# One core, a chain of graph layers: the fetch of sums by source moves from the 23rd to the 37th of 52 groups of row puts, and the K network's way back asks for its tiles from the 40th group on

## What is computed

```python
def get_H(xx):
    z = xx @ W_fc.T
    e = sigmoid(concatenate([z[src], z[dst]], -1) @ W_attn.T)
    w = exp(e - segment_max(e, dst)[dst])
    h = segment_sum(w / segment_sum(w, dst)[dst] * z[src], dst)
    h1 = segment_sum((h @ W_encK.T + b_encK)[src], dst)
    K = _mlp3(h1, ...)                                   # a row for each node
    ue = (h @ W_p1.T + b_p1)[src] + (h @ W_p2.T + b_p2)[dst]
    U = _mlp3(ue, ...)                                   # a row for each edge
    return sum(segment_sum(K[src] * U, dst))
dHdx = jax.grad(get_H)(x)
return dHdx @ J.T - dHdx @ D.T
```

## Time and profile before

| what | us |
|---|---|
| median of 3 runs | 10295.42 |
| lowest and highest | 10291.75, 10301.3 |
| profiled execution, its span | 10295.6 |
| POOL waiting for DVE's join within the puts | 100.26 |
| stretch of the dh1 tiles, first issue to last matmul | 8341.82 to 8866.6 |
| stretch of dsum, first load to the join on PE | 8878.37 to 9073.24 |

### The profile page before, as it was taken

How to read it: one execution, slowest core, us unless ns; L and a number is a source line. 1 busy time by engine, 2 the same in 40 slices (tenths; PEclk the granted TensorE clock), 3 DMA queues, 4 the chain that set the end, 5 groups by cost and what they waited for, 6 DMA issues and landing times. The chain is left out here.

```text
span 10295.6 us, 89257 instructions
## 1 busy us (share of the span) xinstructions
PE 4966.0 (48%) x33607; PEld 2470.1 (24%) x33607; DVE 4608.8 (45%) x6086; ACT 2834.9 (28%) x2203; POOL 6485.8 (63%) x6251
## 2 busy tenths in 40 slices
PE   1000039992467777752666553343330044239955
PEld 0000028882122222210222211233320021023322
DVE  5678777772000010001999400677764410448920
ACT  0111100000000000000999400555556400449910
POOL 4777767776777737777888777787777477310000
PEclk5555555555679999875999866666665566569977
DMA  5666559999999999993655694455559879849978
GB/s 181 226 221 221 183 89 352 350 348 351 405 381 416 386 402 386 385 416 133 201 183 192 232 383 168 161 186 178 178 209 381 310 269 364 316 162 368 359 315 362
DMA packets 987471, 2910.75 MB, mean 283 GB/s; under 512 B 198168, under 2 KB 547467, under 8 KB 936824
## 3 DMA queue, kind: packets, MB, share of 16 engines
q1 hardware_dynamic: 753570, 2579.72, 65.6%
q0 software_dynamic: 213744, 171.38, 6.7%
q10 hardware_dynamic: 19814, 155.07, 3.9%
HBM read 2027.96 MB, written 877.74 MB: 282 GB/s over the span
## 5 line engine op out<-in xcount | busy, mean ns | idle before, releaser
L650 PE MATMUL ps<-arena 128*32 128x400 f32 (+2 forms) x12200 | 2075.4, 694 | 1512.6 <-DMA arena<-cells_w 808.6
L827 PE MATMUL ps<-arena 128*33 128x400 f32 x6400 | 1146.9, 510 | 486.8 <-DVE arena L820 479.3
L650 PEld LDWEIGHTS ps<-arena 128*32 128x32 f32 (+1 forms) x12200 | 629.6, 150 | 2951.7 <-issue 1423.6
L459 POOL DMA_INDIRECT cells_t<-arena x832 | 1081.7, 1300 | 299.6 <-issue 299.6
L456 POOL DMA_INDIRECT arena<-t_a,arena x832 | 953.7, 1146 | 253.5 <-issue 253.5
L459 POOL DMA_INDIRECT cells_c<-arena x832 | 819.8, 985 | 421.4 <-issue 291.4
L459 POOL DMA_INDIRECT cells_w<-arena x832 | 812.1, 976 | 302.9 <-issue 302.9
L459 POOL DMA_INDIRECT sorted<-arena x832 | 808.1, 971 | 301.0 <-issue 301.0
L459 POOL DMA_INDIRECT xd<-arena x832 | 824.5, 991 | 258.2 <-issue 253.3
L456 POOL DMA_INDIRECT arena<-t_kv,idx x832 | 816.8, 982 | 257.9 <-issue 253.3
L668 DVE COPY carry<-ps 64x128 f32<-64x128 f32 (+1 forms) x5 | 1.5, 296 | 1851.0 <-PE ps L650 1851.0
(11 more groups left out here) (526 smaller groups left out, 8221.1 us busy)
## 6 DMA issues: line engine op xcount, KB each, us to landing
arena<-cells_w SPq DMA_DIRECT2D x250, 3200.0 KB
arena<-cells_c SPq DMA_DIRECT2D x100, 3200.0 KB
cells_w<-arena SPq DMA_DIRECT2D x50, 3200.0 KB
cells_c<-arena SPq DMA_DIRECT2D x50, 3200.0 KB
cells_t<-arena SPq DMA_DIRECT2D x50, 3200.0 KB
arena<-cells_c SPq DMA_DIRECT2D x100, 1600.0 KB
arena<-cells_t SPq DMA_DIRECT2D x100, 1600.0 KB
arena<-cells_t SPq DMA_DIRECT2D x50, 3200.0 KB
```

The costliest lines, as they stand in the source:

```text
L459: return pool.indirect_dma_start(table, bass.IndirectOffsetOnAxis(ap=index, axis=0), source, None)
L650: mm = pe.matmul(bank[base + k][g * f:(g + 1) * f, 0:m], rows_of, tile[:, g * width + at:g * width + at + m], start=first, stop=last, skip ...
L827: last = pe.matmul(bank[4 * kind + 2 * h + c][64 * g:64 * g + 33, 0:400], own[:, t, :], moving[:, at:at + 400], start=t == 0, stop=t == NT ...
```

## The change

Two lines change. On POOL the block of step 4 (one joining fetch, one put, 50 fetches) moves behind the 37th group of puts; on SP the group that tile t of dh1 waits for is no longer `26 + t*24//50` (27th to 50th group) but `39 + t*12//50` (40th to 51st group).

```diff
@@ -2299,7 +2299,7 @@ (POOL)
-                if c == 22:
+                if c == 36:
                     ends_pool(pool, "umlp", OS, P, HD)
@@ -2434,7 +2434,7 @@ (SP)
             def amid_puts(t):
-                c = 26 + t * 24 // NT
+                c = 39 + t * 12 // NT
                 sp.wait_ge(S[f"given{c % STAGES}"], 256 * (c // STAGES + 1))
```

## The result

The changed kernel takes 10330.68 us (median of 5 runs, 10327.93 to 10341.69), the kernel before beside it 10294.07 us (10288.81 to 10301.3). The ratio is 1.0037 with a 95% interval of 1.0024 to 1.005: **slower by 37 us**. The forecast was 10338 us, with a range of 10298 to 10368. The profiled execution has a span of 10332.2 us.

What follows compares the result with a forecast made beforehand. Puts bound the stretch, with a 100.26 us POOL wait. Removing it ends puts at 8784; 20 tiles in dsum add 246, then 72.5 and 13.7: crossing 9116, 43 us later, so 10338 us, range 10298 to 10368.

Steps and rivals of the forecast that it cites:

- the K network: PE and DVE work behind the fetched sums: 63.8 us, ending at 8510, its 195 us of delay costing nothing by themselves.
- Between 20.96 and 22.9 I take 22.3: Puts beside unpaced dh1 tiles: 22.3 us a group, 12 groups after 8516, so puts end at 8784.
- I take 2 to 1 in between: Dsum beside tiles: tiles get 267 GB/s, 12.3 us each; dsum gets 133 GB/s, 15.8 us a step.
- rival 1: Dsum beside tiles: packets in turn, 3.1 to 1 for tiles; crossing 9125, +52 us, time 10347; chance 0.30.
- 400 GB/s for both together: Dsum and tiles beside each other: assumed some 400 GB/s in all at a full DMA share.
- the prediction's own sum: Dsum's stretch: 20 tiles take 246 us, 15.6 steps meanwhile, 10.4 left take 72.5, plus 13.7; crossing at 9116.
- Two signs of being wrong: Streams over 415 GB/s: sharing step wrong, time near 10295. Puts ending after 8800: tiles cost more, time longer.
- The step of the first tile: Start of dh1 loads: third group behind the block releases it at 8516, 6 us behind the K network's 8510.
- the top of the range: Whole time: 10368 us, rival 1 at 375 GB/s with the back stage's three reads (4.9 MB) behind it.
- Rival 2: Dsum beside tiles: equal bytes or dsum hardly slowed, crossing +9 to +18 us, time about as before; chance 0.23.
- Rival 3: Tiles 7.8 us each, 431 GB/s kept up for 536 us, crossing 9043, -30 us, time 10265; chance 0.05.
- Rival 4: POOL's wait returns, or the K network sets the first tile, no more than 6 us; no chance of its own.

Runs made afterwards that it cites:

- experiment 1: Kernel before with only the fetch of sums moved behind the 37th group, tiles' counts kept: 10321.18 us against 10292.32, ratio 1.0028.
- experiment 2: Kernel before with only the tiles' counts changed, dh1 tiles waiting for the 40th to 51st group: 10440.57 us, ratio 1.0142.
- experiment 3: Changed kernel with the last 20 of the 50 dh1 tiles loaded only 16 columns wide: 10216.98 us in a single run.
- experiment 4: Changed kernel with dh1 tiles loaded in pieces of 6.4 KB instead of 25.6 KB: 10308.51 us in a single run.
- experiment 6: Kernel before with fetch behind the 28th group, tiles waiting for the 31st to 50th, dh1 pieces of 6.4 KB: 10216.79 us against 10308.97, ratio 0.9915.

## Why the prediction was right, and where it was off

**The mechanism held, in direction and in its steps.** The wait went (2.24 us); the K network moved and cost nothing itself; the first tile came at 8508.8 where 8516 was forecast, 7 us early as the joining fetch was (8371.2, not 8378.6), most of it an offset that is there at the first put already; tiles fell into dsum; dsum's steps stretched until the last tile and then fell back to 7 us; the crossing came at 9112.6 where 9116 was forecast. Experiments 1 and 2 show that each half of the change makes the kernel slower alone, and 3 that the bytes of the tiles are the reason.

**Three terms were off, and their errors nearly cancelled.**

- *"Between 20.96 and 22.9 I take 22.3", the puts beside tiles that aren't paced.* The loads of groups at 8517.62 and 8745.11 are nine groups apart, 25.3 us each, and the last put took 12.42 us to land where it took 5.10. Even with the 7 us of early start dsum began at 8808.1, not 8784: 24 us late. The row that I leaned on, 22.9 us, was from three groups that were held back only now and then. The bounds of 8767 and 8791 for the end of the puts did not hold the value. Experiments 4 and 6 show that the size of the pieces on q1 is the cause: cut to a quarter, the groups take 20.97 and 21.0 us. How POOL's packets get their turn between large ones is not shown.
- *"I take 2 to 1 in between", how dsum and tiles share.* It was about a packet in turn, rival 1's mechanism: 2.9 to 1 in bytes, steps of 19.5 us ((8965.04 - 8867.39)/5, loads of dsum) and tiles 10.1 us apart ((8979.03 - 8816.81)/16), against 15.8 and 12.3. The doubt that I had put against the rule, 15457 packets of q0 against 7056 of q1, stands for q0 (experiment 4), but it says nothing of q10.
- *400 GB/s for both together* was low: 426 in the window 8808 to 8984.

Dsum lasted 304.5 us, not 332: 28 us short. With 17 tiles for 20 the prediction's own sum gives 17 x 12.3 = 209 us, 13.2 steps in it, 12.8 behind it, and 312 us in all. So 20 of the 28 us come from the three tiles that passed PE while the puts were late. This part is no luck: the DMA engines were full from 8509 to 8984, and what a late end of the puts adds ahead of dsum it takes out of dsum. The other 7 us are luck: in that sum the 431 GB/s that 10.1 and 19.5 us make together take some 16 us off, and the share in packets instead of 2 to 1 puts some 9 on. +24 and -28 make the 3.4 us between forecast and crossing.

Two signs of being wrong that the prediction had set for itself came true without what it tied to them. The streams summed to over 415 GB/s, and the sharing step was wrong, but the time was not near 10295. The puts ended after 8800, but the time was not longer than forecast. The step of the first tile had a gap too: the group and the K network were called nearly level, no more than 6 us apart, but without the 40th group the first tile goes out 46 us earlier and the crossing comes 15 us earlier, both counted from the first put (experiment 1). And the top of the range adds 6 us for the three reads of the back stage, for which no working is given.

Rival 1 had the right shares and gave +52 from the same start of dsum; its error was the 400 as well.

**Rival 2, no change,** falls by its own test: steps didn't stay at 7 us. It was nearest in the bytes, since both streams together did come to 426 GB/s. **Rival 3, faster,** needed 431 GB/s for 536 us; measured were 403 and 426 only while tiles ran. **Rival 4** did not occur for the wait; of the first tile's release, the 40th group was the later one, and without it PE starts 16 us earlier (experiment 1).

## What to carry to other kernels

When a wait disappears, work out what the work behind it is late for: here 100 us of POOL's idle time were bought with 310 us, instead of some 156, in which the DMA engines were only a quarter busy, and the bytes that should have moved then fell into a stage that needed the DMA engines itself. A bound by bytes over the whole stretch (here 231 MB in 557 us) tells in one line whether a later start can be made up for. Of the places measured here, the 23rd, 28th and 37th group, the one just behind the end of the wait was the fastest. And a bulk stream beside small urgent transfers can be worth cutting into small pieces: it brought 34 us at the 28th group. Beside dsum it takes from the bulk stream what it gives to the other, so that in experiment 4 the tiles ended last.

## What was unexpected of the hardware

- Large pieces on one queue slow the transfers of the other two, POOL's indirect puts among them: 25.3 us a group and 12.4 us to land the last put with 22.7 KB packets on q1; 20.97 and 4.7 us with 6.2 KB (experiment 4).
- Cutting the pieces in four cost the tiles little: 9.3 us apart beside puts against 9.0, where the puts moved more at the same time, and 423 against 428 GB/s with dsum.
- Reads and writes by two hardware queues together reached 426 to 428 GB/s, level with the 430 of tiles alone, where I had taken 400.
